# An attention and mixture-of-experts layer on one core: other places for side work, and one signal for a couple of heads

## The reference

```
x  : (8, 512, 128) float32          # B = 8 batches, T = 512 tokens, D = 128
xn = (x - mean) / sqrt(var + 1e-5)  # over the last axis

# attention, 16 heads of 8; the rope angle depends on the BATCH index only
q, k, v = xn @ Wq.T, xn @ Wk.T, xn @ Wv.T   (q, k scaled by cos/sin of the batch's angle)
att = softmax(q @ k.T / sqrt(8)) @ v

# feed-forward, 32 experts of 64, a token uses the 6 best of the 4 best groups of 8
scores = sigmoid(xn @ gate_w.T);  sc = scores + e_bias
combine = 2.5 * (scores of the 6 chosen) / their sum, else 0
h   = relu(xn @ up_w.T)**2 * combine
ffn = h @ down_w + relu(xn @ shared_up.T)**2 @ shared_down

out = x + att + ffn
```

## Time and profile before

| | |
|---|---|
| three timed runs | 628.43, 630.48, 630.54 us; median 630.48 |
| the profiled execution | 631.33 us, of it the span 629.5 us, mean granted clock 0.994 |
| PE busy | 619.7 us (98%) |
| DVE, ACT, POOL busy | 417.3, 412.8, 427.4 us (66%, 66%, 68%) |
| chain that ended last | PE 94%, DVE 5%, issue 1% |
| largest waits | DVE for scores 167.3 us; POOL for relu 113.1 us |

### The profile page before, as it was taken

How to read it: one execution, slowest core, us unless ns; L and a number is a source line. 1 busy time by engine, 2 the same in 40 slices (tenths; PEclk the granted TensorE clock), 3 DMA queues, 4 the chain that set the end, 5 groups by cost and what they waited for, 6 DMA issues and landing times.

```text
span 629.5 us, 12299 instructions
## 1 busy us (share of the span) xinstructions
PE 619.7 (98%) x4326; PEld 294.7 (47%) x4326; DVE 417.3 (66%) x1058; ACT 412.8 (66%) x803; POOL 427.4 (68%) x512
## 2 busy tenths in 40 slices
PE   8999999999999999999999999999999999999997
PEld 6443455544545445444444545444454444444443
DVE  7868775757758676676857677586766868565402
ACT  4658667667666666766767677666766666666664
POOL 5840368667786678866788667876776766667653
PEclk9979999999999999999999999999999999999999
DMA  4165753745435354552447454363545633343420
GB/s 145 45 183 162 171 119 84 232 102 150 104 68 201 73 151 106 173 165 47 121 93 234 102 125 109 77 203 84 136 106 143 189 69 94 86 101 68 103 68 17
DMA packets 51997, 75.68 MB, mean 120 GB/s; under 512 B 5984, under 2 KB 19168, under 8 KB 51936
## 3 DMA queue, kind: packets, MB, share of 16 engines
q1 hardware_dynamic: 51916, 74.90, 44.7%
q10 hardware_dynamic: 20, 0.00, 0.0%
HBM read 56.14 MB, written 18.35 MB: 118 GB/s over the span
## 4 chain that ended last, share of the span: by engine, by line
PE 94%; DVE 5%; issue 1%; DMA 0%; ACT 0%; DVEq 0%
PE acc L1201 21%; PE pv L1195 19%; PE st L1225 10%; PE st L1165 8%; PE upb L1225 8%; PE sc L1154 7%; PE upb L1165 4%; PE st L1170 3%; DVE nmax L918 2%; PE st L1070 2%; PE upb L1170 2%; PE st L1113 2%; PE st L1107 1%; PE st L1137 1%; PE upb L1113 1%; PE st L1120 1%
## 5 line engine op out<-in xcount | busy, mean ns | idle before, releaser
L918 DVE TENSOR_REDUCE nmax<-sc 128x1 f32<-128x512 f32 x512 | 328.1, 686 | 170.1 <-PE sc L1154 167.3
L553 POOL TENSOR_TENSOR gated<-gate_at,relu 128x512 f32<-128x512 f32 x111 | 142.0, 1279 | 113.7 <-ACT relu L700 113.1
L695 ACT ACTIVATE probs<-st 128x512 f32<-128x512 f32 x352 | 199.3, 595 | 28.6 <-PE st L1170 18.0
L557 POOL TENSOR_TENSOR g<-gated,relu 128x512 f32<-128x512 f32 x111 | 141.2, 1272 | 16.2 <-POOL gated L553 0.4
L1170 PE MATMUL st<-stacks 32*128 32x512 f32 x352 | 149.0, 581 | 0.0
L1154 PE MATMUL sc<-stacks 32*128 32x512 f32 x512 | 137.1, 495 | 2.1 <-DVE nmax L918 1.8
L1201 PE MATMUL acc<-dn,g 128*128 128x128 f32 x1016 | 137.8, 279 | 0.8 <-issue 0.8
L1195 PE MATMUL pv<-probs,v_aug 128*32 128x512 f32 x1024 | 136.4, 605 | 0.1
L1201 PEld LDWEIGHTS acc<-dn,g 128*128 128x128 f32 x1016 | 125.1, 191 | 20.8 <-issue 18.8
L695 ACT ACTIVATE probs<-upb 128x512 f32<-128x512 f32 x160 | 95.2, 595 | 25.2 <-PE st L1170 20.0
L1165 PE MATMUL st<-m_rows,ones 3*128 3x512 bf16 x352 | 99.0, 386 | 0.2 <-ACT sh L677 0.2
(11 more groups left out here) (188 smaller groups left out, 580.6 us busy)
## 6 DMA issues: line engine op xcount, KB each, us to landing
gate_at<-gate_rows SPq DMA_DIRECT2D x62, 512.0 KB, 6.3
stacks<-q_stack SPq DMA_DIRECT2D x30, 256.0 KB, 6.8
stacks<-k_stack SPq DMA_DIRECT2D x30, 256.0 KB, 6.9
q_stack<-qk_parts SPq DMA_DIRECT2D x28, 256.0 KB, 6.4
k_stack<-qk_parts SPq DMA_DIRECT2D x28, 256.0 KB, 5.5
x_res<-in_x SPq DMA_DIRECT2D x8, 256.0 KB, 7.3
out<-y SPq DMA_DIRECT2D x8, 256.0 KB, 7.1
m_rows<-m_parts SPq DMA_DIRECT2D x95, 4.0 KB
```

Of the source, the lines that this page charges most:

```text
L553: nc.gpsimd.tensor_tensor(gated[:, u % 2, :], gate_at[:, group % RING, u % GATES, :], relu[:, u % RELUS, :], ALU.mult).then_inc(gated_read ...
L557: nc.gpsimd.tensor_tensor(g[:, u % 2, :], gated[:, u % 2, :], relu[:, u % RELUS, :], ALU.mult).then_inc(g_ready, 1)
L695: nc.scalar.activation(probs[:, u % 2, h, :], ring_b("st", u * QUAD + h)[:], ACT.Exp).then_inc(probs_ready, 1)
L918: nc.vector.tensor_reduce(out=nmax[:, s % 2, at:at + 1], in_=sc_b[tile % SC_BANKS][:], op=ALU.max, axis=AXX, negate=True).then_inc(s_read, 1)
```

## The change

1. **Side work in units 0 to 6** (below `FIRST_LAG` = 7): on PE (`side_work`), on ACT (`side_out`) and in the ring's order, the side operation stands between the two couples, behind `pv(u - 1)`. From unit 7 on it stays behind couple 1.
2. **Signals.** `t_done` is replaced by `couple_done`. In units 0 to 7 (`LONE` = 8) the last product of a couple increments it once, and each score still increments `s_done`. From unit 8 on only the couple's last matmul does: its last score, or its last product where it has none. All exponentials wait for the couple; row maxima of tiles from unit 8 on wait for the couple too.
3. **DVE's order in batches 1 to 7.** The residual add goes from the head of unit 2 to the end of unit 1, behind the attention output. Router pieces and statistics all stand behind the maxima of couple 1, by one table. Batch 0 keeps its order.

```diff
-        SUM_UNIT, Y_UNIT = 2, 3
+        SUM_UNIT, Y_UNIT = 1, 3
-        ROUTE_MID, ROUTE_END = {0: 0, 3: 3, 4: 4, 7: 6, 8: 7}, {1: 1, 2: 2, 6: 5, 8: 8, 10: 9}
+        ROUTE_AT = {0: (0,), 2: (1,), 3: (2,), 4: (3, 4), 5: (5,), 6: (6,), 7: (7,), 8: (8,), 11: (9,)}
...
                 order += [("st", u * QUAD), ("st", u * QUAD + 1)]
+                second = [("st", u * QUAD + 2), ("st", u * QUAD + 3)]
...
-                order += [("st", u * QUAD + 2), ("st", u * QUAD + 3)]
+                if u >= FIRST_LAG:
+                    order += second
...
+                if u < FIRST_LAG:
+                    order += second
                 if not last:
                     order += [("up", u)]
...
             def exponent(u, h):
-                act.wait_ge(t_done, u * QUAD + h + 1)
+                act.wait_ge(couple_done, u * 2 + h // 2 + 1)
...
                 exponent(u, 1)
                 if kt == 0 and q and q % PAIR == 0:
                     att_evac(q // PAIR - 1)
+                if u < FIRST_LAG:
+                    side_out(u)
...
                 exponent(u, 3)
...
+                if u >= FIRST_LAG:
+                    side_out(u)
...
-                dve.wait_ge(s_done, tile + 1)
+                if COUPLE_OF.get(tile, 0) <= 2 * LONE:
+                    dve.wait_ge(s_done, tile + 1)
+                else:
+                    dve.wait_ge(couple_done, COUPLE_OF[tile])
...
+                for tile in SC_AT[u, 1]:
+                    row_max(tile)
+                if kt == ATT_KT and q and q % PAIR == 0:
+                    att_out(q // PAIR - 1)
                 if n == SUM_UNIT and b:
                     add_residual(b - 1)
...
+                if b and b + 1 < B:
+                    for piece in ROUTE_AT.get(n, ()):
+                        route(b + 1, piece)
+                if b and b + FIRST_X < B:
                     if n == STATS_UNIT:
                         stats_of(b + FIRST_X)
...
                 for h in (2 * k, 2 * k + 1):
-                    weights_product(u, h)
+                    last = weights_product(u, h)
+                if u < LONE:
+                    last.then_inc(couple_done, 1)
+                    for tile in SC_AT[u, k]:
+                        score(tile).then_inc(s_done, 1)
+                    return
                 for tile in SC_AT[u, k]:
-                    score(tile)
+                    last = score(tile)
+                last.then_inc(couple_done, 1)
...
+                if u < FIRST_LAG:
+                    side_work(u)
+                couple(u, 1)
+                if u >= FIRST_LAG:
+                    side_work(u)
```

More of the change, by code:

```diff
@@ L81, in place_scores @@
             SC_AT[u, couple] = list(range(at, at + n))
+            COUPLE_OF.update((tile, u * 2 + couple + 1) for tile in SC_AT[u, couple])
             at += n
@@ L1012, in _ @@
                         moments(b + FIRST_X).then_inc(var_ready, 1)
[L1013 to L1020, removed]
             add_pair(0)
@@ L1153, in score @@
                 wait(pe, s_read, tile - SC_BANKS + 1)
-                nc.tensor.matmul(sc_b[tile % SC_BANKS][:], stacks[rows_of(h), s % NQ, 0, qt * P:(qt + 1) * P],
-                                 stacks[rows_of(h), s % NQ, 1, :], start=True, stop=True).then_inc(s_done, 1)
+                return nc.tensor.matmul(sc_b[tile % SC_BANKS][:], stacks[rows_of(h), s % NQ, 0, qt * P:(qt + 1) * P],
+                                        stacks[rows_of(h), s % NQ, 1, :], start=True, stop=True)
             def weights_max(u, h):
@@ L1169, in weights_product @@
                 j, kt = u // TT % NQ, u % TT
-                nc.tensor.matmul(ring_b("st", u * QUAD + h)[:], stacks[rows_of(h), j, 1, kt * P:(kt + 1) * P],
-                                 stacks[rows_of(h), j, 0, :], start=False, stop=True).then_inc(t_done, 1)
+                return nc.tensor.matmul(ring_b("st", u * QUAD + h)[:], stacks[rows_of(h), j, 1, kt * P:(kt + 1) * P],
+                                 stacks[rows_of(h), j, 0, :], start=False, stop=True)
             def couple(u, k):
@@ L1315, in _ @@
                     shared_down(b, SHDOWN_UNIT.index(n))
+            pe.wait_ge(blank_ready, 1)
+            warm(WARM_FIRST, sc_b[0])
+            pe.wait_ge(id_ld, 16)
+            transpose_x(0)
+            warm(WARM_COPY, sc_b[0])
+            pe.wait_ge(w_ld, NW1 * 16)
+            pe.wait_ge(xnT_half, 1)
+            pe.wait_ge(xnT_ready, 1)
+            for i, (w, at) in enumerate(FIRST_PIECES):
+                project_rows(0, w, at, first_b[i])
+            logits(0)
+            warm(WARM_ROWS, sc_b[0])
+            for i in range(TILES // 2):
+                score(2 * i).then_inc(s_done, 1)
+                score(2 * i + 1).then_inc(s_done, 1)
+                beside(*BESIDE[i // 2], slice(i % 2 * (T // 2), (i % 2 + 1) * (T // 2)))
+            for kind, i in CUT_WAIT:
+                beside(kind, i)
+            pe.wait_ge(v_ready, 1)
+            max_transpose(0)
+            for i in range(FIRST_AHEAD // 2):
+                score(TILES + 2 * i).then_inc(s_done, 1)
+                score(TILES + 2 * i + 1).then_inc(s_done, 1)
+                if i < len(BEHIND):
+                    beside(*BEHIND[i])
+            pe.wait_ge(m_ready, 1)
+            pe.wait_ge(sh_relu, 1)
+            pe.wait_ge(qk32_ready, 2)
+            for u in range(UNITS):
+                b, n, kt, q = u // SLICES, u % SLICES, u % TT, u // TT
+                couple(u, 0)
+                if u:
+                    pv(u - 1)
+                if u == UNITS - 1:
+                    expert_up(u)
+                if u < FIRST_LAG:
[3 more added lines that the diff above has]
+                    side_work(u)
                 if u == 0:
```

114 lines of the change are left out of this document (46 added, 68 removed).

## The result

| | before | after |
|---|---|---|
| time, median (lowest to highest) | 630.51 us (628.43 to 630.95, 4 runs) | 623.37 us (623.17 to 624.28, 4 runs) |
| ratio, 95% interval | | 0.9896 (0.9872 to 0.9920) |
| profiled execution, its span | 631.33, 629.5 us | 623.35, 621.5 us |
| unit 1, unit 8, unit 127 begin, against before | | 4.01, 4.81, 8.02 us earlier |

The changed kernel is 1% faster: 7.1 us between the medians, 7.98 between the two profiled executions. A unit is taken to begin with its first maxima matmul on the PE timeline. Read that way, 4.8 us are won ahead of unit 8, another 3.17 in unit 2 of batches 1 to 6, and outside these two places no unit's length changes by more than 0.03 us.

A forecast was written before the change was run, and what follows sets the result against it. PE, busy 619.7 of 629.5 us, was taken as the bound. Gains of 5.1 + 3.2 + 0 = 8.3 us gave 623.0 us for a profiled execution, 622.2 for the median, range 619.3 to 627.4.

The forecast's parts named there:

- Part 1: Units 0 to 6: side operations moved between the couples bring the first down product 5.1 us earlier, bounds 2.0 and 5.7.
- PE's lead behind unit 2: Start: the row maximum behind stack 2 comes 4.2 us earlier, and the stage from there to 56.13 keeps that shift.
- may take back some tenths: Early units: ACT has about 4.1 us of work a unit, so it may reduce the start's gain by some tenths.
- Part 2: Unit 2 of batches 1 to 6: moving residual adds and router pieces ends its stalls, 3.2 us, bounds 2.0 to 4.0.
- The stall left standing: Batch 6, unit 105: a four-element DVE add beside POOL's multiplication took 1.15 us, the unit 1.2 us longer; expected to stay.
- Part 3: Unit 8 on: one signal a couple saves PE nothing and readers have cover; 0 us, with -1 to +1.
- From the profiled execution to the median: Whole run: 0.85 us taken off the profiled execution's forecast, 623.0, to give the median's, 622.2.
- A: Start gains less: the clock falls as before or a load is late; 2 to 3.5 us stays, 624.5; chance 0.17.
- B: Start gains nothing: the gate chain is held by its DMAs, not the transpose; 3.2 us left, 627.3; chance 0.08.
- C: Couples: the single signal comes late and every couple 1's second score waits; slower, 633; chance 0.06.
- D: Couples from unit 8 on: the increments do cost PE time, 20 us, giving 602; chance 0.02.
- E: Whole change: moved pieces meet POOL elsewhere, stalls move, DVE paces the start as before; 630; chance 0.05.

The follow-up runs named there:

- e6_warm: The kernel before with six dummy 128x128x128 matmuls between the couples of unit 0, no real work moved: 627.98 us, ratio 0.9972.
- part 1 alone: The kernel before with only the side work of units 0 to 6 moved between the couples: 626.61 us, ratio 0.9951.
- part 3 alone: The kernel before with only the signals changed, one a couple from unit 8 on: 629.95 us against 629.52, ratio 1.0000.

## Why the prediction was right, and where its terms were off

**Part 1, size 5.1, measured 4.84 us** (at unit 17; 4.81 at unit 8). Unit 1 came 4.01 us earlier (said: 4.1), the row maximum behind stack 2 at 38.80 (said: about 38.6), and the score in front of it did wait for stack 2. That the clock stays up and gives most of the gain, e6_warm and part 1 alone show. The term that was mis-sized is PE's lead behind unit 2, which I kept at 4.2 us: it is 3.8 behind unit 3. So the gate transpose came 4.67 us earlier (57.90 to 53.23) and not 5.1, and the first down product at 62.79 instead of 62.4: PE's 3.8 us and the 0.9 that it had waited there make the 4.73. That POOL's gating came 5.11 us earlier, as the sum said, is luck: the way from the transpose to the gating took 7.82 us instead of 8.26, and in the two further profiles of the kernel before it took 7.94 and 8.47. Of unit 3, which is 4.92 us long instead of 4.55, the timeline gives the parts: V half to the next work 0.74 us (44.00 to 44.74) instead of 0.64, up product 1.06 (45.52 to 46.58) instead of 0.96, and couple 0 lasts 0.18 us more because its scores wait for row maxima:

```profile
44.00 0.81 PE L1132 MATMUL upb<-wvg,xnT 128*128 128x160 f32 x4
44.74 0.39 PE L1190 MATMUL st<-m_rows,ones 3*128 3x512 bf16 x2
...
45.52 1.12 PE L1256 MATMUL upb<-xnT,up 128*128 128x512 f32 x2
46.58 0.52 PE L1190 MATMUL st<-m_rows,ones 3*128 3x512 bf16 x2
```

I had costed the moved operations at nothing beyond their clock; the V half and the up product, taken apart by a couple, cost 0.1 us more each, and so does the gate transpose (0.54 us to the next work, 53.23 to 53.77, instead of 0.44). ACT, which "may take back some tenths", shows too. In the list of weight loads' waits, from 32 to 67 us, the maxima matmuls (L1190) wait for exponentials (L702) for 4.7 us in seven waits. Before, over the same units (36 to 71 us), it was 3.0 us in four waits. A weight load waits ahead of its matmul, so this is mostly not PE's own time, and how much of the missing 0.26 us it is stays open.

**Part 2, size 3.2, measured 3.17 us.** Right in size and in each place. The comparison with batch 7 was the argument that carried: a unit in the same kernel that already had the new order. What the text called two moves is one, though: piece 1 does it, the residual nothing.

**The stall left standing** stayed at 5.63 us for unit 105, as said, with its cause as said.

**Part 3, size 0, measured 0** (to within some 0.7 us, by the interval). Right, by rows 11. One sign was wrong: the maximum doesn't start 0.03 us later but 0.045 earlier (0.68 after the couple's start, instead of 0.725). Before, the update of the semaphore for the first score came as the third of the couple, behind those of two products; now there is one update, and nothing stands ahead of it. The exponential starts 0.025 later, not 0.10. The Trainium skill, page "TensorE: Matmul & The Clock Gate", section "The cost: per-tile semaphore tail", has increments on concurrent matmuls serialize at some 26 ns each. The records agree in kind (34 ns apart, below), but the tail runs behind the couple: with it in PE's way the total would have been 18 us lower, by the estimate in the prediction, and it is 0.

**From the profiled execution to the median.** I took off 0.85 us for both kernels alike. The forecast for the profiled execution, 623.0, came out at 623.35; the median at 623.37, where I said 622.2. Of the 1.2 us between the forecast time and the median some 0.85 are this step, and 0.35 the sum: a good part of what makes executions of the kernel before differ is the low clock near its start, and the change takes that away from nearly all of them. An offset that lies in a stretch the change rewrites doesn't carry over. For the same reason the parts measured less between medians (7.1, and 2.9 for part 1 alone) than between the profiles (7.98 and 4.71): the profiled execution of before was the costliest of all its executions.

**The rivals.** A (the clock falls all the same) fell with the windows, B (the gate chain held by its loads) with the gating 5.11 us earlier, C and D with part 3 alone, E with the units' lengths.

## What to carry to other kernels

Where PE is sparsely used near the start, look at the granted clock of the stretch behind as well: the low clock cost some 3 us here, and moving ready work there gained more than dummies did. One profile shows one place and length of the low clock; a second and a third showed others. To cost a changed order, look for a place in the same trace that already has it. And before an offset between a profiled execution and the median is carried over, find where the executions differ.

## What the runs showed of the hardware

- **Increments.** Before, the four semaphore updates of a couple stand 0.635, 0.669, 0.704 and 0.738 us after its start, 34 ns apart (two products, then two scores), though its matmuls run side by side; a single one on the last score stands at 0.660. The couple takes 0.55 us with four increments, with two and with one.
- **The low clock differs in length and place between executions.** In the three profiles of the kernel before it lasted 6.83, 6.83 and 3.41 us, from 31.25, 29.6 and 31.8 us on. PE's gap ahead of couple 1's scores was 0.62, 0.18 and 0.54 us and ended at 30.70, 30.76 and 30.48, so in the second profile the clock fell before the gap, and the gap can't be what started it there; nor does it in e1_signals_only, where it fell at 29.3 and that gap is missing. With 128-row matmuls between the couples, dummies or work, the clock stayed at 1.00 through the units of all eight profiles. What lets it fall stays open.
- **A neighbour sets the time of a tiny instruction.** The timelines of DVE, POOL and PE, units 104 and 105 of after:

```profile
512.86 1.03 POOL L542 TENSOR_TENSOR sh<-sh 128x512 f32<-128x512 f32 x1
513.17 0.87 DVE L915 TENSOR_TENSOR tmp<-sc,sig 128x128 f32<-128x128 f32 x1
...
514.25 1.28 POOL L560 TENSOR_TENSOR gated<-gate_at,relu 128x512 f32<-128x512 f32 x1 [0.36 <-ACT relu L707]
...
514.39 1.16 DVE L917 TENSOR_SCALAR wsum<-wsum 128x4 f32<-128x4 f32 x1
...
516.34 0.49 PE L1179 MATMUL sc<-stacks 32*128 32x512 f32 x1 [0.69 <-DVE nmax L935]
```

  DVE's product ends (514.04) just after POOL's square (513.89), and its four-element add ends (515.55) with POOL's multiplication (515.53), which began 0.14 us before it. Where the router piece stands two units later the add takes 0.17 us. With router piece 1 moved back, the multiplication waited for its load and the add slipped in ahead by 0.10 us:

```profile
517.62 0.17 DVE L917 TENSOR_SCALAR wsum<-wsum 128x4 f32<-128x4 f32 x1
517.72 1.28 POOL L560 TENSOR_TENSOR gated<-gate_at,relu 128x512 f32<-128x512 f32 x1 [0.61 <-DMA gate_at<-gate_rows]
```

  The Trainium skill, page "GPSIMD Engine Reference", section 1 (Specifications), speaks of contention with VectorE over SBUF; the rows agree and give it a price here: the DVE instruction is held until POOL's has ended. The add has only one input in SBUF, so of the page's two conditions (a 2-port mode, two SBUF inputs) only the first could be its; whether it ran in such a mode the rows don't show. That it is so for every such instruction isn't shown: row maxima ran beside POOL's work at their usual 0.69 us.
